# Spreading the dequantisation of packed 4-bit weights over the set-up of a transformer-block kernel

## The chip, the core and the metric

The kernel runs on one core of a Trainium2 chip. The metric is the device time in microseconds (us) of one execution. Before the change it is 905.2 us, the median of 3 runs (905.16 to 906.35).

The names used below: PE is TensorE, DVE is VectorE, ACT is ScalarE, POOL is GpSimd, SP is SyncE (here only a queue that issues DMAs). L985 is line 985 of the kernel.

## What is computed

One block on `x` of 32 x 64 tokens, 512 wide:

```python
# layer norm, cross attention of x on ctx with 16 heads of 4 x 8 channels,
# channels mixed by a 4x4 matrix per head, scores per channel group m
qh = interfere(proj(ln(x), Wq, bq)); kh, vh = the same of ctx with Wk, Wv
w  = softmax(einsum('bhqdm,bhkdm->bhqkm', qh, kh) / sqrt(8), axis=3)
x  = x + einsum('bhqkm,bhkdm->bhqdm', w, vh).reshape(...) @ Wo.T + bo
# feed forward with 4-bit weights: 8 values per uint32, groups of 128 rows
W[i, j] = scale[g[i], j] * (nibble[i, j] - (zero[g[i], j] + 1))
h  = silu(ln(x) @ W_gate) * (ln(x) @ W_up)       # 512 -> 1376
x  = x + h @ W_down                              # 1376 -> 512
```

`g` is an input (one group number per row), 4 groups for gate and up, 10 for down. Everything is kept in pairs of 16-bit numbers: a high half and a low half with the rest, so that a product is three matmuls.

## The kernel before, in words

Tokens are taken in 8 chunks of 256. The loop body runs the attention of chunk c and, between its steps, slices of the feed forward of chunk c-1. There are 20 places ("slots") for such slices in a chunk: two ahead of the scores, four in each of four batches, four at the tail. The order of work on each engine is written out by hand (`pe_chunk`, `act_chunk`, `dve_chunk`, `pool_chunk`), and the engines meet at semaphores. An engine works its own list strictly in order.

Chunk 0 has no feed forward of a chunk before, so its slots hold the dequantisation of the feed-forward weights, which stay in SBUF from then on. Chunk 1 can't start its slices before the last unit is done (`d_lo`).

**Set-up** (`sync_setup`, `pe_setup`, `act_setup`, `dve_setup`, `pool_setup`). A small matrix per weight block is built from `interference` (DVE, to L972). PE turns the biases with it (L403, L406) and folds it into Wk, Wv, Wq (L420); Wo is put in another column order by 32 copies on DVE (L985) and turned on PE (L423). ACT brings the folded weights back to SBUF (L737). DVE takes the largest absolute value of each weight (L988), of the scales (L994, L995) and of the eight chunks of context (L998). POOL takes the maximum over all partitions (`partition_all_reduce`, L1297), DVE works out scale factors from it, powers of two, up to L1045 (`scale_ready`). Then ACT and DVE write the high (`act_whi`, L749) and low (`dve_wlo`, L1059) halves of the four weights, and keys, values and queries of chunk 0 are projected. POOL makes the one-hot matrices of the group numbers (`pool_hot`, L1320 to L1324) and the rests of the scale tables (L1301 to L1310); ACT rounds those tables (L758), DVE unpacks the zero points (`dve_zeros`, L1067, L1070).

**A unit of the dequantisation** is a block of 128 rows by up to 512 columns; there are ND = 35 (24 of gate and up, 16 of them 512 and 8 of them 352 columns wide, and 11 of down). Unit n goes through

1. DVE: shift and mask the nibbles, SBUF to SBUF (`dve_dequant_int`, L1083),
2. ACT: convert to bf16 (`act_dequant_conv`, L794),
3. PE: three matmuls; scale rows into PSUM bank UB (L443), minus the zero rows (L444) plus the nibbles (L446) into bank GB,
4. ACT: GB times a power of two into SBUF (`act_dequant_scaled`, L777),
5. DVE: that times UB (`dve_dequant_w`, L1094),
6. ACT: the high half (`act_dequant_hi`, L767), 7. POOL: the low half (`pool_dequant_lo`, L1334).

Matmuls of unit n wait for step 5 of unit n-1, since there is one pair of banks:

```python
reached(e, S["d_w"], n)
```

The packed weights come in 14 pieces of up to 688 KB over two buffers; a piece is loaded when the units of the piece two before it are through step 1.

Of the kernel before, what the change touches and what calls it, by code (L numbers as in the profile page):

```python
# [22 lines left out]
P = 128  # L23
# [60 lines left out]
TICKS = ND + 3  # L84
FIRST_SLOT = 2
TICK_ENDS = [0] * FIRST_SLOT + [TICKS * (k + 1) // (SLICES - FIRST_SLOT) for k in range(SLICES - FIRST_SLOT)]

def ticks(slot):
    return range(TICK_ENDS[slot - 1] if slot else 0, TICK_ENDS[slot])  # L90

# [12 lines left out]
def build(nc, x, ctx_in, Wq, bq, Wk, bk, Wv, bv, interference, amp, Wo, bo,  # L104
          qw_gu, qz_gu, sc_gu, gi_gu, qw_d, qz_d, sc_d, gi_d, out):
    with ExitStack() as stack:
# [16 lines left out]
        small = sb("small", [P, 124], F32)  # L123
# [66 lines left out]
        wop = [take(2048, F32) for _ in range(KB)]  # L190
        bvx = take(2048, F32)

        inter_all, inter_own, own = wop[0][:, 0:HEADS * SUP * SUP], wop[1][:, 0:HEADS * SUP * SUP], wop[2][:, 0:4 * SUP]
# [20 lines left out]
        scgu = words(WD_f, 2 * INTER, 2 * INTER)  # L214
        o = [0]

        def temp(n):
            o[0] += n
            return words(WGU_f, o[0] - n, n)
        rest_gu, rest_d, scd = temp(2 * INTER), temp(DM), temp(DM)  # L220
        zint = temp(2 * INTER).bitcast(U32)
        zraw_gu, zraw_d = temp(2 * INTER // 8).bitcast(U32), temp(DM // 8).bitcast(U32)
        gidx_gu, gidx_d, hot_f = temp(DM), temp(INTER), temp(INTER)
# [23 lines left out]
        BMASK = small[:, 108:124].rearrange("p (w v k) -> p w v k", w=2, v=2)  # L247
        GM = small[:, 100:101]
# [6 lines left out]
            "const_loaded", "bo_loaded", "sc_loaded", "gi_loaded", "z_loaded", "qw_loaded0", "qw_loaded1",  # L255
# [5 lines left out]
            "sc_high", "sc_rest", "hot_ready", "z_ready",  # L261
# [53 lines left out]
        def sync_chunk(e, c, first=False):  # L315
            if first:
                load_ctx(e, 1)
            if not is_last(c):
                e.wait_ge(S["xres_ready"], 2 * c + 2)
                e.wait_ge(S["xln_ready"], 2 * c + 2)  # L320
                e.dma_start(xin, x_d[c + 1]).then_inc(S["x_loaded"], 16)
            reached(e, S["pv_done"], SLOTS * c)
            v_dmas(e, c, first)
            if first:
                for i in range(2, len(PIECES)):
                    e.wait_ge(S["d_int"], units_before(i - 1))
                    load_piece(e, i)
# [18 lines left out]
        def sync_setup(e):  # L346
# [5 lines left out]
            e.dma_start(zraw_gu[0:GROUPS_GU, :], qz_gu).then_inc(S["z_loaded"], 16)  # L352
            e.dma_start(zraw_d[0:GROUPS_D, :], qz_d).then_inc(S["z_loaded"], 16)
            for w in WORDER:
                e.dma_start(wraw[w], (Wq, Wk, Wv, Wo)[w].rearrange("(g p) n -> p g n", p=P)).then_inc(S[f"w_loaded{w}"], 16)
                if w == WORDER[0]:
                    e.dma_start(gidx_gu[0:96, :].bitcast(I32), gi_gu.partition_broadcast(96)).then_inc(S["gi_loaded"], 16)
                    e.dma_start(gidx_d[0:96, :].bitcast(I32), gi_d.partition_broadcast(96)).then_inc(S["gi_loaded"], 16)

            e.wait_ge(S["sc_zeroed"], 1)  # L360
            for i in range(PARTS):
                e.dma_start(scgu[32 * i:32 * i + GROUPS_GU, :], sc_gu).then_inc(S["sc_loaded"], 16)
                e.dma_start(scd[32 * i:32 * i + GROUPS_D, :], sc_d).then_inc(S["sc_loaded"], 16)

            for c in range(NCHUNK):
                e.dma_start(cmax_st[:, c].rearrange("p (t n) -> p t n", t=TILES), c_d[c]).then_inc(S[f"ctxm_loaded{c}"], 16)
            e.dma_start(cin, c_d[0]).then_inc(S["ctx_loaded"], 16)
            e.dma_start(xin, x_d[0]).then_inc(S["x_loaded"], 16)
            load_piece(e, 0)
            load_piece(e, 1)  # L370
            e.dma_start(bo_row[:, :], bo.partition_broadcast(P)).then_inc(S["bo_loaded"], 16)

# [24 lines left out]
        def pe_setup(e):  # L397
            e.wait_ge(S["t_ready"], 2)
            e.wait_ge(S["pool_const"], 1)

            for i in range(2):
                for g in range(KB):
                    mm = e.matmul(bank[4][:, 4 * i + g:4 * i + g + 1], tmat[:, g, :], BQR[:, 4 * i + g:4 * i + g + 1],  # L403
                                  start=True, stop=True)
            for g in range(KB):
                mm = e.matmul(bank[5][:, g * P:(g + 1) * P], bvx[:, g * P:(g + 1) * P], tmat[:, g, :],  # L406
                              start=True, stop=True)
            mm.then_inc(S["bias_done"], 1)
            for i, w in enumerate(WORDER):
                banks = bank[4 * (i % 2):4 * (i % 2) + 4]  # L410
                e.wait_ge(S[f"w_loaded{w}"], 16)
                reached(e, S["fold_evicted"], i - 1)
                if i == 1:
                    e.wait_ge(S["bias_evicted"], 1)
                if w == 3:
                    e.wait_ge(S["wo_permuted"], 1)
                for cb in range(KB):
                    for g in range(KB):
                        if w < 3:
                            mm = e.matmul(banks[cb][:, g * P:(g + 1) * P], wraw[w][:, g, cb * P:(cb + 1) * P],  # L420
                                          tmat[:, g, :], start=True, stop=True)
                        else:
                            mm = e.transpose(banks[cb][:, g * P:(g + 1) * P], wop[g][:, cb * P:(cb + 1) * P], ident[:, :])  # L423
                mm.then_inc(S["fold_done"], 1)

        def pe_dequant(e, n):
# [6 lines left out]
            pick = slice(blk * P, blk * P + m)  # L436
            if n == 0:
                e.wait_ge(S["hot_ready"], 2)
                e.wait_ge(S["z_ready"], 2)
                e.wait_ge(S["sc_high"], 6)  # L440
                e.wait_ge(S["ident16_ready"], 1)
            reached(e, S["d_w"], n)
            e.matmul(UB[0:m, 0:cols], hot[0:64 + groups, pick], sc3[0:64 + groups, c0:c0 + cols], start=True, stop=True)  # L443
            e.matmul(GB[0:m, 0:cols], hot[0:groups, pick], z[0:groups, c0:c0 + cols], start=True, stop=False)  # L444
            e.wait_ge(S["d_conv"], n + 1)
            e.matmul(GB[0:m, 0:cols], ident16[0:m, 0:m], wbf[n % 2][0:m, 0:cols], start=False, stop=True).then_inc(S["d_gathered"], 1)  # L446

        def t_bank(c, name):

            if isinstance(c, int) and c < 0:  # L450
                return {"cT0": AB[2], "cT1": AB[3], "xT0": GB, "xT1": UB}[name]
# [81 lines left out]
        def pe_chunk(e, c, first=False, last=False):  # L533
# [4 lines left out]
            def ffn_slice(k):  # L538
                if first:
                    for n in ticks(k):  # L540
                        pe_dequant(e, n - 1)
# [7 lines left out]
            if first:  # L549
                e.wait_ge(S["fold_evicted"], 4)  # L550
                for t in range(TILES):
                    pe_transpose_tile(e, -1, f"cT{t}", cin, S["ctx_loaded"], 16)
# [5 lines left out]
            if first:  # L558
                e.wait_ge(S["wlo_done"], 2)
                for t in range(TILES):  # L560
                    pe_rows(e, 2, t, AB[2 + t], cxT, S["proj_done"])
                for i in range(TILES):
                    pe_transpose_tile(e, -1, f"xT{i}", xln, S["xln_ready"], i + 1)
                e.wait_ge(S["wlo_done"], 3)
                e.wait_ge(S["t_lo"], t_at(-1, "xT1"))
            else:
# [162 lines left out]
        def act_setup(e):  # L729
            e.wait_ge(S["bias_done"], 1)  # L730
            e.activation(bv_row[:, :], bank[5][:, :], ACT.Copy)
            e.activation(bqk[:, :, :].rearrange("p a b -> p (a b)"), bank[4][:, 0:8], ACT.Copy).then_inc(S["bias_evicted"], 1)
            for i, w in enumerate(WORDER):
                e.wait_ge(S["fold_done"], i + 1)
                e.wait_ge(S["wmax_done"], i + 1)
                for cb in range(KB):
                    ins = e.activation(wraw[w][:, cb], bank[4 * (i % 2) + cb][:, :], ACT.Copy)  # L737
                ins.then_inc(S["fold_evicted"], 1)
                if i == 1:
                    act_scale_part(e, 0)  # L740
# [3 lines left out]
            act_whi(e, 1)  # L744

# [5 lines left out]
        def act_scale_part(e, i):  # L751

            if i == 0:
                e.wait_ge(S["sc_loaded"], 32 * PARTS)
            else:
                e.wait_ge(S["sc_rest"], 2 * i)
# [723 lines left out]
```

## Time and profile before

| | |
|---|---|
| median of 3 runs | 905.2 us |
| the profiled execution | 906.32 us, of which the core's span in the profile is 904.6 us |
| set-up, to the first scores of chunk 0 | 0 to 108.8 us of the span |
| chunk 0 from its scores to the first matmul of the next chunk | 108.8 to 240.3 us |
| the other seven chunks and the last feed forward | 240.3 to 904.6 us |
| PE busy | 85% of the span |
| DVE, ACT, POOL busy | 56%, 48%, 36% |

A row of a timeline gives the start, the time taken, the engine, the line, the operation, what it writes and reads, the shapes, and in brackets the idle time of the engine ahead of it with what ended it. Neighbouring instructions of a line are merged (x32), their time then is from the first's start to the last's end.

### The profile page before, as it was taken

To read this page: it belongs to the slowest core of one execution; us is meant where nothing else is said; L and a number is where in the kernel's file an instruction comes from. 1 tells how busy PE (TensorE), PEld (TensorE's weight loads), DVE (VectorE), ACT (ScalarE), POOL (GpSimd) and SP (SyncE) were. 2 spreads that over 40 slices of the span, in tenths; PEclk is the share of its full clock that TensorE was granted. 3 is DMA by queue.
4 is the path that set the end of the run, shared out by engine and by line. 5 is a ranking of instruction groups with operands and counts; after the bars stand their busy time and mean duration, and the time that the engine had idled before them with its cause. 6 is when DMAs were issued, how large, how long until landed. Compare 5 with 4: busy or idle time off the path is not lost.

```text
span 904.6 us, 23874 instructions
## 1 busy us (share of the span) xinstructions
PE 772.6 (85%) x9953; PEld 562.3 (62%) x9953; DVE 510.2 (56%) x1013; ACT 438.3 (48%) x806; POOL 326.8 (36%) x290
## 2 busy tenths in 40 slices
PE   5306457766799999999999999999999999999898
PEld 5303323322278857876787778677857885787484
DVE  6987745554465646655574556456645663644421
ACT  1426355676365526662555455454635462655120
POOL 6732324555314530543064114412431352144220
PEclk9758655565599999999999999999999999999999
DMA  8900113222101011002100110011001100010000
GB/s 248 292 23 1 50 32 89 69 56 63 32 25 28 3 49 50 3 3 71 28 2 14 60 28 3 13 60 28 2 21 52 28 2 25 3 27 3 24 1 23
DMA packets 20702, 36.98 MB, mean 41 GB/s; under 512 B 3374, under 2 KB 7602, under 8 KB 20592
## 3 DMA queue, kind: packets, MB, share of 16 engines
q1 hardware_dynamic: 20604, 35.48, 13.5%
q8 instruction: 85, 1.39, 0.6%
q14 instruction: 13, 0.11, 0.0%
HBM read 26.56 MB, written 4.19 MB: 34 GB/s over the span
## 4 chain that ended last, share of the span: by engine, by line
PE 67%; DVE 15%; ACT 8%; issue 6%; DMA 2%; SPq 1%; DVEq 0%; ACTq 0%; POOL 0%
PE bank L511 16%; PE bank L526 13%; PE bank L482 9%; PE bank L492 9%; PE bank L644 4%; DVE nmf L1166 4%; PE bank L638 3%; PE bank L661 3%; ACT arena L849 3%; PE bank L619 2%; PE bank L459 2%; DVE arena L1094 2%; DMA arena<-in_L_xattn_Wo 2%; DVE arena L985 2%; PE bank L443 2%
## 5 line engine op out<-in xcount | busy, mean ns | idle before, releaser
L511 PE MATMUL bank<-arena,WGU 128*128 128x256 f16 (+1 forms) x2112 | 247.0, 274 | 1.4 <-DVE arena L709 1.4
L511 PEld LDWEIGHTS bank<-arena,WGU 128*128 128x128 f16 (+1 forms) x2112 | 206.2, 100 | 27.5 <-DVE arena L709 1.6
L1368 POOL TENSOR_TENSOR arena<-arena 128x512 f16<-128x512 f32 x128 | 147.0, 1173 | 190.5 <-ACT arena L856 190.5
L482 PE MATMUL bank<-arena,WT 128*128 128x256 f16 x768 | 91.3, 281 | 40.4 <-DVE arena L709 39.1
L526 PE MATMUL bank<-WD,arena 128*128 128x512 f16 (+1 forms) x528 | 121.1, 379 | 0.0
L849 ACT ACTIVATE arena<-bank,small 128x512 f32<-128x512 f32 x128 | 89.1, 776 | 58.3 <-PE bank L644 58.3
L1355 POOL TENSOR_TENSOR arena<-arena 128x512 f16<-128x512 f32 (+1 forms) x48 | 51.7, 1077 | 172.2 <-ACT arena L829 172.2
L482 PEld LDWEIGHTS bank<-arena,WT 128*128 128x128 f16 x768 | 76.9, 101 | 54.6 <-issue 43.1
L492 PE MATMUL bank<-WT,arena 128*128 128x512 f16 x384 | 88.0, 387 | 1.8 <-DVE arena L707 1.8
L526 PEld LDWEIGHTS bank<-WD,arena 128*128 128x128 f16 (+1 forms) x528 | 49.4, 98 | 53.2
L1166 DVE TENSOR_REDUCE nmf<-bank 128x8 f32<-128x512 f32 x128 | 79.4, 682 | 4.4 <-PE bank L619 4.2
L809 ACT ACTIVATE arena<-bank,bqk,small 128x256 f32<-128x256 f32 x64 | 38.4, 601 | 82.2 <-PE bank L482 82.2
L856 ACT ACTIVATE arena<-arena 128x512 f16<-128x512 f32 x128 | 71.9, 628 | 0.0
L813 ACT ACTIVATE arena<-bank,small 128x256 f16<-128x256 f32 x128 | 67.9, 608 | 0.0
L492 PEld LDWEIGHTS bank<-WT,arena 128*128 128x128 f16 x384 | 38.0, 99 | 47.4 <-issue 4.2
L1118 DVE SCALAR_TENSOR_TENSOR arena<-arena,small 128x512 f16<-128x512 f32 x64 | 45.2, 748 | 37.5 <-ACT arena L813 37.5
L644 PE MATMUL bank<-nmT,sel 32*128 32x128 f32 x1024 | 61.6, 317 | 0.0
L1125 DVE RECIPROCAL rinv<-bank 128x16 f32<-128x16 f32 x64 | 16.3, 255 | 78.1 <-PE bank L661 78.1
L1341 POOL TENSOR_TENSOR rstd<-vareps,small 128x1 f32<-128x1 f32 x32 | 19.6, 622 | 100.2 <-DVE vareps L1104 93.1
L1146 DVE SCALAR_TENSOR_TENSOR arena<-arena,small,bank 128x512 f32<-128x512 f32 (+1 forms) x48 | 33.6, 699 | 38.3 <-PE bank L511 37.1
L1142 DVE SCALAR_TENSOR_TENSOR arena<-arena,bank 128x512 f32<-128x512 f32 (+1 forms) x48 | 30.7, 639 | 41.9 <-ACT arena L825 41.9
L661 PEld LDWEIGHTS bank<-arena 128*128 128x128 f16 x1536 | 46.9, 97 | 9.7 <-issue 1.8
(157 smaller groups left out, 1068.8 us busy)
## 6 DMA issues: line engine op xcount, KB each, us to landing
arena<-in_L_ffn_qweight_gu SPq DMA_DIRECT2D x8, 688.0 KB, 5.4
arena<-arena SPq DMA_DIRECT2D x32, 144.0 KB, 3.0
WT<-in_ctx SPq DMA_DIRECT2D x8, 512.0 KB, 15.1
arena<-in_ctx SPq DMA_DIRECT2D x8, 512.0 KB, 3.7
arena<-in_x SPq DMA_DIRECT2D x8, 512.0 KB, 3.6
out_y<-arena SPq DMA_DIRECT2D x16, 256.0 KB, 2.1
arena<-in_L_ffn_qweight_down SPq DMA_DIRECT2D x10, 256.0 KB, 3.4
arena<-in_L_xattn_Wk SPq DMA_DIRECT2D x1, 1024.0 KB, 6.6
```

The costliest lines, as they stand in the source:

```text
L482: mm = e.matmul(jb[:, g2 * TOK:(g2 + 1) * TOK], WT[:, w, sp, kb, g * P:(g + 1) * P], src[:, mp, kb, :], start=(n == 0), stop=(n == 11))
L492: mm = e.matmul(jb[:, :], src[:, sp, kb, t * P:(t + 1) * P], WT[:, w, mp, kb, :], start=(n == 0), stop=(n == 11))
L511: mm = e.matmul(pb[0:m, i * TOK:(i + 1) * TOK], WGU[:, sp, kb, half * INTER + fb * P:half * INTER + fb * P + m], x2T[:, mp, kb, :], start= ...
L526: mm = e.matmul(pb[:, :], hT[0:m, sp, fb, t * P:(t + 1) * P], WD[0:m, mp, fb, :], start=(n == 0), stop=(n == 3 * FB - 1))
L644: mm = e.matmul(AB[a][:, i * P:(i + 1) * P], sel[rows, i, :], nmT[rows, :], start=False, stop=True)
L661: mm = e.matmul(JB[0][:, at:at + 2 * VCOLS], phl[:, a, part, i * P:(i + 1) * P], vv[:, b, :, 4 * i + a, v0:v0 + VCOLS], start=(n == 0), st ...
L813: ins = e.activation((qm, km)[w][:, 0, NB * g:NB * g + NB, v, :], src.rearrange("p (n t) -> p n t", n=NB), ACT.Identity, bias=BMASK[:, w, ...
L849: e.activation(pring[:, a, :], AB[a][:, :], ACT.Exp, bias=LIFT, scale=KSM).then_inc(S["exp_done"], 1)
L856: e.activation(phl[:, a, 0, :], pring[:, a, :], ACT.Copy).then_inc(S["p_hi"], 1)
L1166: e.tensor_reduce(nmf[:, a, 0:8], AB[a][:, :].rearrange("p (n k) -> p n k", n=8), AX_X, ALU.max, negate=True).then_inc(S["max_done"], 1)
L1355: e.tensor_tensor(flat(1), hbuf[0:m, u % 2, 0:cols], flat(0), ALU.subtract).then_inc(S["h_lo"], 1)
L1368: e.tensor_tensor(phl[:, a, 1, :], pring[:, a, :], phl[:, a, 0, :], ALU.subtract).then_inc(S["p_lo"], 1)
```

## The change

- The dequantisation starts in the set-up. Instead of two units or so in each of 18 slots, the steps are spread over named places: 26 ticks in 15 places of the set-up and ahead of the scores, and 14 in the slots of chunk 0, three in each batch and two at the tail.
- Units below 23 with an even number use a second pair of PSUM banks (JB), so their matmuls wait for step 5 of unit n-2. The folds of the weights then have one set of four banks, where they had two in turn.
- Step 2, the conversion to bf16, moves from ACT to POOL. Step 5 is three ticks behind step 1, where it was one.
- The tables of gate and up are made wide (128 and 32 partitions in place of 4) on DVE and sent to their rows by 12 and 4 small DMAs. Their one-hot matrix is made on DVE, that of down stays on POOL in four parts between the folds.
- The maximum over the scales gets a `partition_all_reduce` of its own, early.
- The 32 copies that reorder Wo go from DVE to ACT.
- The loads are put in another order: pieces of packed weights between the weights and the chunks of context, each behind a wait on step 1.

```diff
+PLACES = ["tables", "bias", "fold0", "fold1", "fold2", "fold3", "ctx2", "ctx4", "ctx6", "ctx8", "scales", "w0", "w1",
+          "keys", "values"] + list(range(SLICES))
+TICKS_AT = {"tables": 2, "bias": 2, "fold0": 2, "fold1": 2, "fold2": 2, "fold3": 2, "ctx2": 1, "ctx4": 1, "ctx6": 1,
+            "ctx8": 1, "scales": 2, "w0": 2, "w1": 2, "keys": 2, "values": 2}
+BATCH_TICKS = [slot[j] for slot in IN_BATCH for j in (0, 2, 3)] + AT_TAIL[:2]
+TWO_PAIRS = sum(TICKS_AT[p] for p in PLACES[:PLACES.index("values") + 1]) - 3
...
@@ def sync_setup
+            load_piece(e, 0)
+            load_w(e, 1)
...
+            load_piece(e, 1)
+            e.wait_ge(S["sc_zeroed"], 2)
+            e.wait_ge(S["wide_ready"], 1)
+            for i in range(PARTS):
+                for g in range(GROUPS_GU):
+                    e.dma_start(sc3_gu[32 * i + g:32 * i + g + 1, :], sc3w[32 * g:32 * g + 32, i, :]).then_inc(S["sc_table"], 16)
+            e.wait_ge(S["zwide_ready"], 1)
+            for g in range(GROUPS_GU):
+                e.dma_start(z_gu[g:g + 1, :], zw[8 * g:8 * g + 8, :]).then_inc(S["z_table"], 16)
+            load_w(e, 2), load_w(e, 0)
+            load_next_piece(e, 2)
+            load_w(e, 3)
+            load_ctx_max(e, 0), load_ctx_max(e, 1)
+            load_next_piece(e, 3)
...
+        def pe_ticks(e, place):
+            for n in ticks(place):
+                pe_dequant(e, n - 2)
+        def dq_banks(n):
+            return (JB[0], JB[1]) if n < TWO_PAIRS and n % 2 == 0 else (GB, UB)
@@ def pe_dequant
-            reached(e, S["d_w"], n)
+            reached(e, S["d_w"], n - 1 if n < TWO_PAIRS else n)
@@ def act_setup
             for i, w in enumerate(WORDER):
+                if w == 3:
+                    act_permute(e)
                 e.wait_ge(S["fold_done"], i + 1)
                 e.wait_ge(S["wmax_done"], i + 1)
...
+                act_ticks(e, f"fold{i}")
+            for place in ("ctx2", "ctx4", "ctx6", "ctx8"):
+                act_ticks(e, place)
+            act_scale_part(e, 2)
+            act_ticks(e, "scales")
             e.wait_ge(S["scale_ready"], 1)
             act_whi(e, 0)
             act_hi(e, -1, "cT0"), act_hi(e, -1, "cT1")
+            act_ticks(e, "w0")
             act_whi(e, 1)
+            act_ticks(e, "w1")
+        def act_ticks(e, place):
+            for n in ticks(place):
+                act_dequant_scaled(e, n - 2)
+                act_dequant_hi(e, n - 4)
@@ def dve_setup
+            dve_tables(e)
+            dve_ticks(e, "tables")
             link(e, e.tensor_copy(T1, smalli[:, 4:5]))
...
+        def dve_tables(e):
...
+            e.wait_ge(S["maxq_all"], 1)
...
+        def dve_ticks(e, place):
+            for n in ticks(place):
+                dve_dequant_int(e, n)
+                dve_dequant_w(e, n - 3)
@@ def pool_setup
-            pool_hot(e, GROUPS_D, INTER, gidx_d, hot_d)
-            pool_hot(e, GROUPS_GU, DM, gidx_gu, hot_gu)
+            e.wait_ge(S["maxq_ready"], 1)
+            e.partition_all_reduce(MRQ, MXQ, P, ABSMAX).then_inc(S["maxq_all"], 1)
...
+            pool_ticks(e, "tables")
+            pool_ticks(e, "bias")
+            for i in range(4):
+                pool_hot_d(e, i)
+                pool_ticks(e, f"fold{i}")
...
+            for place in ("ctx2", "ctx4", "ctx6"):
+                pool_ticks(e, place)
             e.wait_ge(S["max_ready"], 1)
             e.partition_all_reduce(MR, MX, P, ABSMAX).then_inc(S["max_all"], 1)
+            pool_ticks(e, "ctx8")
             pool_ln(e, "x", 0)
+            pool_ticks(e, "scales")
...
+        def pool_ticks(e, place):
+            for n in ticks(place):
+                pool_dequant_conv(e, n)
+                pool_dequant_lo(e, n - 5)
+        def pool_dequant_conv(e, n):
...
+            e.wait_ge(S["d_int"], n + 1)
+            reached(e, S["d_gathered"], n - 1)
+            e.tensor_copy(wbf[n % 2][0:m, 0:cols], wint[n % 2][0:m, 0:cols]).then_inc(S["d_conv"], 1)
```

Step 1 of unit n still waits for the conversion of unit n-2 (`d_conv`), as before.

## Rows read from the trace of the kernel before

**Rows 1.** Busy time of each engine by stretch, with the granted clock

```profile
core 0: us, PE busy (x) PEld busy (x) DVE busy (x) ACT busy (x) POOL busy (x), PEclk, DMA share, GB/s
...
108.80:240.30 131.50, 82.76 (x838) 38.81 (x838) 69.17 (x129) 80.84 (x149) 58.09 (x53) 0.56 0.22 59
```

**Rows 2.** Timeline of DVE in the set-up

```profile
22.19 14.38 DVE L985 COPY arena<-arena 128x64 f32<-128x64 f32 x32 [1.35 <-DMA arena<-in_L_xattn_Wo]
36.49 2.27 DVE L988 TENSOR_REDUCE maxima<-arena 128x1 f32<-128x2048 f32 x1
...
42.93 9.08 DVE L998 TENSOR_REDUCE small<-WT 128x1 f32<-128x1024 f32 x8
...
59.43 0.49 DVE L1045 TENSOR_SCALAR bv_row<-bv_row,small 128x512 f32<-128x512 f32 x1
...
88.19 6.77 DVE L1191 TENSOR_TENSOR arena<-arena 128x512 f16<-128x512 f32 x2
```

**Rows 3.** Chain that ended last, 108.8 to 240.3 us: shares, then start, time, piece

```profile
by line: DVE arena L1094 11.7%; PE bank L443 10.7%; ACT arena L777 10.2%; PE bank L446 10.0%; PE bank L444 9.6%; DVE nmf L1166 7.2%; issue 6.7%; PE bank L644 6.5%; ACT arena L849 4.5%; PE bank L638 4.3%; DVE arena L1083 3.4%; PE bank L619 3
...
231.19 0.70 ACT arena L777
...
234.37 0.70 ACT arena L777
```

**Rows 4.** Timeline of POOL in the set-up

```profile
4.36 2.41 POOL L1293 MEMSET WD<- 96x2752 f32 x1
...
19.56 3.11 POOL L1322 TENSOR_TENSOR WGU<-WGU 96x1376 f32<-96x1376 f32 x1
22.76 4.86 POOL L1323 TENSOR_SCALAR WGU<-WGU 96x1376 f32<-96x1376 f32 x1
27.72 3.82 POOL L1324 TENSOR_SCALAR arena<-WGU,small 96x1376 bf16<-96x1376 f32 x1
31.61 0.64 POOL L1320 CAST WGU<-WGU 96x512 f32<-96x512 int32 x1
...
60.00 1.12 POOL L1341 TENSOR_TENSOR rstd<-vareps,small 128x1 f32<-128x1 f32 x2 [7.14 <-issue]
```

**Rows 5.** Single lines: shortest, median and longest duration in ns

```profile
L985 DVE COPY arena<-arena x32: 195/202/4866, 22.2 to 36.4; 128x64 f32<-128x64 f32 x32
...
L1083 DVE TENSOR_SCALAR arena<-arena,smalli x35: 394/486/1474, 112.7 to 233.4; 128x512 uint32<-128x512 uint32 x26, 128x352 uint32<-128x352 uint32 x8, 96x512 uint32<-96x512 uint32 x1
...
L1059 DVE SCALAR_TENSOR_TENSOR WT<-arena,small,WT x4: 2335/2352/6647, 62.0 to 84.5; 128x2048 f16<-128x2048 f32 x4
```

**Rows 6.** Groups by line, 0 to 215 us: busy us, mean ns of one, idle before

```profile
L1334 POOL TENSOR_TENSOR WGU<-arena,WGU 128x512 f16<-128x512 f32 (+1 forms) x24 | 27.0, 1136 | 48.1 <-ACT WGU L767 48.1
L777 ACT ACTIVATE arena<-bank,small 128x512 f32<-128x512 f32 (+1 forms) x27 | 17.5, 650 | 23.3 <-PE bank L446 23.3
L1094 DVE TENSOR_TENSOR arena<-arena,bank 128x512 f32<-128x512 f32 (+1 forms) x27 | 17.2, 636 | 31.9 <-ACT arena L777 31.9
L446 PE MATMUL bank<-arena,ident 128*128 128x512 bf16 (+1 forms) x28 | 14.9, 532 | 0.0
...
L749 ACT ACTIVATE WT<-arena,small 128x2048 f16<-128x2048 f32 x4 | 8.1, 2020 | 17.5 <-DVE bv_row L1045 17.5
```

**Rows 7.** Timeline of PE: starts of its stages

```profile
9.05 3.57 PE L403 MATMUL bank<-small,arena 128*128 128x1 f32 x16 [9.05 <-DVE arena L972]
...
14.33 11.94 PE L420 MATMUL bank<-arena 128*128 128x128 f32 x96
...
96.30 8.11 PE L482 MATMUL bank<-arena,WT 128*128 128x256 f16 x48 [12.57 <-DVE arena L709]
108.80 1.47 PE L619 MATMUL bank<-arena 32*128 32x128 f16 x48 [4.38 <-DVE arena L1118]
...
240.29 7.79 PE L492 MATMUL bank<-WT,arena 128*128 128x512 f16 x24 [1.77 <-DVE arena L707]
```

**Rows 8.** Timeline of SP's queue: the issue of one load

```profile
12.21 0.29 SPq L362 DMA_DIRECT2D WD<-in_L_ffn_scales_gu  x1
```

More of the change, by code:

```diff
@@ L83, with ticks @@
 PARTS = 3
[L84 to L90, printed above, removed]
+TICKS = ND + 5
+PLACES = ["tables", "bias", "fold0", "fold1", "fold2", "fold3", "ctx2", "ctx4", "ctx6", "ctx8", "scales", "w0", "w1",
[3 more added lines that the diff above has]
+BATCH_TICKS = [slot[j] for slot in IN_BATCH for j in (0, 2, 3)] + AT_TAIL[:2]
+assert sum(TICKS_AT.values()) + len(BATCH_TICKS) == TICKS
+TICKS_AT.update((k, 1) for k in BATCH_TICKS)
+TWO_PAIRS = sum(TICKS_AT[p] for p in PLACES[:PLACES.index("values") + 1]) - 3
+def ticks(place):
+    before = sum(TICKS_AT.get(p, 0) for p in PLACES[:PLACES.index(place)])
+    return range(before, before + TICKS_AT.get(place, 0))
 def width(block):
@@ L189, in build @@
         eye4 = take(16, F32)
+        early = [take(2048, F32) for _ in range(KB)]
+        bvx = take(2048, F32)
+        inter_all, inter_own, own = early[0][:, 0:HEADS * SUP * SUP], early[0][:, 256:512], early[1][:, 0:4 * SUP]
+        zraw_d = early[1][:, 4 * SUP:4 * SUP + DM // 8].bitcast(U32)
+        zint_d, scd = early[2].bitcast(U32), early[3]
+        rest_d = take(2048, F32)
         wop = [take(2048, F32) for _ in range(KB)]
-        bvx = take(2048, F32)
-        inter_all, inter_own, own = wop[0][:, 0:HEADS * SUP * SUP], wop[1][:, 0:HEADS * SUP * SUP], wop[2][:, 0:4 * SUP]
         take, pos = carver(max(pos[0], body0_end))
@@ L247, in build @@
         BMASK = small[:, 108:124].rearrange("p (w v k) -> p w v k", w=2, v=2)
+        MXQ, MRQ, BDQ, SCQ = (small[:, 124 + 2 * i:126 + 2 * i] for i in range(4))
         GM = small[:, 100:101]
@@ L539, in ffn_slice @@
                 if first:
-                    for n in ticks(k):
-                        pe_dequant(e, n - 1)
+                    pe_ticks(e, k)
                     return
@@ L833, in act_slot @@
             if first:
-                for n in ticks(k):
-                    act_dequant(e, n)
+                act_ticks(e, k)
             else:
@@ L869, in act_chunk @@
                 act_whi(e, 2)
+                act_ticks(e, "keys")
             else:
@@ L1155, in dve_slot @@
             if first:
-                for n in ticks(k):
-                    dve_dequant_int(e, n)
-                    dve_dequant_w(e, n - 1)
+                dve_ticks(e, k)
             else:
@@ L1327, in pool_dequant_lo @@
+        def pool_dequant_conv(e, n):
+            if not 0 <= n < ND:
+                return
+            _, (blk, down, c0, cols) = DQ_UNITS[n]
+            m = width(blk) if down else P
+            e.wait_ge(S["d_int"], n + 1)
+            reached(e, S["d_gathered"], n - 1)
+            e.tensor_copy(wbf[n % 2][0:m, 0:cols], wint[n % 2][0:m, 0:cols]).then_inc(S["d_conv"], 1)
         def pool_dequant_lo(e, n):
@@ L1358, in pool_slot @@
             if first:
-                for n in ticks(k):
-                    pool_dequant_lo(e, n - 3)
+                pool_ticks(e, k)
             else:
@@ L1370, in pool_chunk @@
         def pool_chunk(e, c, first=False, last=False):
+            if first:
+                pool_ticks(e, "keys")
+                e.wait_ge(S["bo_loaded"], 16)
+                e.wait_ge(S["wlo_done"], 3)
+                pool_xres(e, 0)
+                pool_ticks(e, "values")
             pool_slot(e, c, 0, first)
```

279 lines of the change are left out of this document (164 added, 115 removed).

## The prediction

> **What bounds the kernel now.** I read the busy times by stretch first. From 108.8 to 240.3 us the clock granted to PE is 0.56, its lower level of 1.2 GHz most of the time, and no engine is busy for two thirds of the stretch [rows 1]: a chain bounds it, not an engine. The chain of waits names it: steps 5, 3, 4 and 1 of the dequantisation (L1094, L443, L777, L446, L444, L1083) hold 55.6% of the stretch [rows 3], 73.1 us or 2.09 us for each of the 35 units. Where nothing else runs, a unit takes 3.18 us, from one L777 to the next [rows 3]. The other 58.4 us are chunk 0's own attention. The set-up ahead of it is bounded by DVE: from 22.2 us it reorders Wo (14.4 us), takes maxima until 52.0 us and has the scale factors at 59.9 us [rows 2]; the query projection starts at 96.3, the scores at 108.8 and the next chunk at 240.3 us [rows 7]. After that the change touches nothing, so it is worth what it moves the mark at 240.3 us.
>
> The third thing to see is how DVE and POOL get in each other's way. A copy of 202 ns (median) takes 4866 ns once [rows 5], and it lies beside POOL's L1323 of 4.86 us [rows 4]. L1059 takes 6.65 us once and else 2.35, L1083 0.49 and up to 1.47 us [rows 5]; L1191 takes 6.77 us for two [rows 2], where L1094 of the same size takes 0.64 each [rows 6]. Such a DVE operation waits until POOL's ends. Reductions don't show it. The 32 copies are 6.4 us of work and the rest is waiting.
>
> **What goes.** The attention of chunk 0 keeps 12 units of 35 (units 23 to 34). At 2.09 us each they are 25.1 us on its chain; 58.4 + 25.1 = 83.5 us in place of 131.5, so 48.0 us go. I checked the share: the tick ahead of the maximum's turn adds steps 1 and 5 and three matmuls, the last one of a batch waits for exponentials, step 4 and step 5, some 6 us a batch. The bounds are nothing on the chain (another 25.1 us gone) and 3.18 us each (13.1 us less gone). The middle is nearest to what the stretch shows.
>
> **What comes, stage by stage.** Prices: on PE a unit is three matmuls of 0.53, 1.6 us; on ACT steps 4 and 6 are 0.65 each, 1.3 us; on DVE steps 1 and 5 are 0.4 and 0.6, 1.0 us [rows 5, 6] without waiting; on POOL step 7 is 1.1 us [rows 6]. The conversion on POOL isn't in the trace. Its nearest row is the cast of 96x512 in 0.64 us; the bounds are that and the two-input operation of step 7, 1.14 us; I take 0.6 as a mean with the narrow units, so a tick is 1.7 us of POOL.
>
 The zero fills end near 5.6 us (L1293 is halved), a swap and the reduction end at 13.1, and the swap back at 20.2 us. DVE is held at `maxq_all` until 13.1, then has 2 us of factors and first ticks and the 4.8 us of matrices that stood ahead of L403; PE gets its bias matmuls at 20.2 us, not 9.05, and needs 5.3 us for them [rows 7]. Unit 0 is through step 5 at 25.5 + 1.6 + 0.65 + 0.65 = 28.4 us.
>
> *To the end of the context maxima.* DVE's work from there: four weight maxima of 2.28 us, 9.1 for the context [rows 2], 2.1 of small maxima and zero points, 11 ticks of 1.0: 31.3 us. Its waits: the one-hot matrix of down is four POOL operations of 4.9, 3.1, 4.9 and 3.8 us [rows 4], one at each fold. A step 1 (or the table cast) that comes behind their start waits 2.6, 1.9, 4.5 and 2.6 us by my laying out, and three more times it waits for a step 7 of 1.1; step 5 waits 0.8 us for ACT once and 4.9 us at the last fold, behind the reordering of Wo (32 small copies on ACT, 3 to 6.4 us, 5 taken, near the 202 ns of a copy on DVE [rows 5]), four more of PE's transposes and 2.1 of eviction. Together 20.6. The maxima end at 28.4 + 31.3 + 20.6 = 80.3 us, where they end at 52.0 now. The 14.4 us that DVE sheds are in this.
>
> *The scale factors.* POOL is done some 1.6 us before DVE, then swaps (7.1) and reduces (0.4): 86.2 us, 4 us after the layer-norm statistics of DVE that would cover it. The factors take 5.8 us (59.9 less 52.0, less 2.1 of statistics): 92.0 us, against 59.9.
>
> *To the query projection.* Now 36.4 us. Two waits of DVE for POOL go, since the operations behind them are gone: 4.3 (L1059) and 5.5 (L1191). Added: 3.7, since ACT's first high half stands behind unit 15, whose conversion waits for the swap back; 0.9 of L1059 behind a step 7; a pair of ticks at w0, 1.0 + 1.6 + 1.3 = 3.9; at w1 2.6 and the second weight's halves, 2.0 and 2.35 [rows 5, 6], which now stand ahead of PE's key projection, 7.0; at the keys 3.9 and a L1059 of 2.35, 6.2; at the values 2.0 + 1.6 + 1.3 and 1.2 of halves that were hidden, 6.1; and 1.5 for two-input operations of DVE that meet POOL. 36.4 - 9.8 + 29.3 = 55.9 us: the query projection starts at 147.9 us and the scores, 12.5 us later as now, at 160.4. That is 51.6 later.
>
> *At no cost.* The 16 table DMAs take SP about 0.3 us each [rows 8], 5 us, and hold back two weight loads that DVE wants after 35 us. Loads behind waits on step 1 (the last weight at 24 us, contexts from 24 to 64 us) each come over 5 us ahead of their maxima. If the first conversions slip by more than that, SP's queue is what is late next. One set of banks for the folds costs PE a wait for the eviction, which lies beside DVE's reduction.
>
> **Sum.** +51.6 and -48.0 give +3.6 us on the mark at 240.3 us. The profiled execution took 906.32 us, its span 904.6; the median is 905.2, 1.1 below that execution. 905.2 + 3.6 = 908.8 us. The change takes a chain of 3 us a unit away and puts in another of 2.2 us a unit, paced by POOL and DVE in turn.
>
> At two places the Trainium skill prices what I took from rows. GPSIMD Engine Reference, section 2.1, says that the first call after new code has been loaded pays about 6 us with no visible instruction. The row has 7.14; with 6 us on the three swaps that lie on the path, the sum would be near 905.4, no change. The same page, section 3.1, has 769 ns as its best case for 512 elements of one input; the row of the cast has 640, and with the page's figure on the 14 conversions that DVE waits for, the sum would be 2 us higher.
>
> **Rivals.** *A, as summed*, 900 to 917 us. *B, the waits of DVE for POOL are mostly missed.* Who comes first has the port: step 1 comes 0.4 us behind the 4.9 us operation at the third fold in my laying out, so a slip of half a microsecond turns 4.5 us to nothing, and it may free the steps behind. Without the 11.6 and 3.3 us of these waits it is 893.9 us. For it: DVE then runs two units ahead; against: POOL still has to come round, and L1083 waits often even with POOL under half busy. *C, slower: POOL paces the set-up more than laid out.* Place: conversions and swaps. If the conversion is 1.14 us, 14 on the path cost 7 us more; and the first two swaps fall in the time in which the loads are heaviest, where one now falls with nothing to show its length; 5 us for these. 920.8 us. It decides from a conversion of 0.9 us on. *D, the 12 units left are all exposed*, at 3.18 us: 921.9 us. For it: with one tick a slot each unit waits for a step on another engine's list; against: the exponentials and maxima cover some. That the early units aren't done early can't be: each engine's list forces it. That the second pair of banks does nothing is likely in part, and changes nothing in the sum, since POOL and DVE pace the ticks.
>
> **How the numbers follow.** A 0.38, B 0.32, C 0.20, D 0.10. Of A's 0.38, 0.08 lie below 903.4, 0.12 within 0.2% (1.8 us, what a measurement of this kernel can tell from no change) and 0.18 above. So faster 0.40, same 0.12, slower 0.48. The range reaches past B and C by the bounds of the conversion and the waits, 890 to 924; A's own is 900 to 917.
>
> **What would show it.** In the profile after: an idle of about 7 us on POOL ahead of the first conversion and twice around the second all-reduce; the conversion near 0.6 us; step 1 with a median above 0.5 us and some of 2 to 5 us in the folds; `scale_ready` near 92, the query projection near 148, the scores near 160 and the next chunk's first row matmuls near 244 us; 84 us of attention with 12 units. Wrong I am if the scores come before 150 us (B) or after 170 (C), or if the attention of chunk 0 takes 95 us (D) or 70.

## The result, and the profile after

The changed kernel takes 923.95 us (median of 4 runs, 923.25 to 924.24) against 905.47 us before (4 runs): ratio 1.0201, 95% interval 1.0184 to 1.0219. It is slower by 18.5 us. The forecast was 908.8 us, slower, in a range of 890 to 924. The result lies 0.05 us inside the upper end of that range and outside the 900 to 917 of the sum itself, where rival D stood with 921.9 us.

The busy times by stretch of the kernel after, cut at its first scores and at the first row matmuls of the next chunk, where [rows 1, 7] have 108.8 and 240.3 us:

```profile
core 0: us, PE busy (x) PEld busy (x) DVE busy (x) ACT busy (x) POOL busy (x), PEclk, DMA share, GB/s
0.00:162.30 162.30, 80.84 (x347) 47.87 (x348) 99.70 (x215) 65.28 (x134) 68.07 (x76) 0.71 0.43 121
162.30:257.60 95.30, 47.45 (x765) 30.28 (x765) 37.22 (x80) 37.69 (x68) 39.98 (x41) 0.57 0.07 20
257.60:922.50 664.90, 647.27 (x8844) 487.92 (x8844) 352.84 (x700) 316.20 (x598) 214.08 (x202) 0.99 0.08 23
```

The set-up is 53.5 us longer (162.3 for 108.8), chunk 0's attention 36.2 us shorter (95.3 for 131.5), and the rest 664.9 us where it was 664.3. So the change is worth what it moves the mark at 240.3 us, which is at 257.65 us now: 17.4 us of the 17.9 in the span. The clock in the attention is 0.57 in place of 0.56; it plays no part.

The timeline of DVE in the set-up after, for [rows 2]:

```profile
17.15 0.62 DVE L1051 COPY arena<-bv_row 128x128 f32<-128x128 f32 x4
...
27.36 7.23 DVE L1178 TENSOR_SCALAR arena<-arena 10x64 uint32<-10x64 uint32 x8
...
42.50 2.54 DVE L1194 TENSOR_SCALAR arena<-arena,smalli 128x512 uint32<-128x512 uint32 x1
...
52.10 4.13 DVE L1194 TENSOR_SCALAR arena<-arena,smalli 128x352 uint32<-128x352 uint32 x1
...
61.05 3.32 DVE L1194 TENSOR_SCALAR arena<-arena,smalli 128x352 uint32<-128x352 uint32 x1
72.31 0.52 DVE L1205 TENSOR_TENSOR arena<-arena,bank 128x352 f32<-128x352 f32 x1 [7.94 <-ACT arena L870]
...
82.24 2.34 DVE L1069 TENSOR_REDUCE small<-WT 128x1 f32<-128x1024 f32 x2
...
95.96 0.48 DVE L1120 TENSOR_SCALAR bv_row<-bv_row,small 128x512 f32<-128x512 f32 x1
```

Step 1 (L1194) takes 0.48 us (0.40 for 352 columns) where POOL is quiet and 2.5, 4.1 and 3.3 us behind three of the one-hot operations. Eight tiny operations on the zero points take 7.2 us behind the first; unhindered they took 0.93. The other side is the timeline of POOL after, for [rows 4]:

```profile
11.48 0.37 POOL L1405 PARTITION_ALL_REDUCE small<-small  x1 [5.89 <-issue]
20.30 1.14 POOL L1407 TENSOR_TENSOR arena<-arena 96x512 f32<-96x512 f32 x1 [8.45 <-issue]
22.17 1.17 POOL L1456 CAST arena<-arena 128x512 bf16<-128x512 uint32 x2 [0.73 <-ACT arena L849]
...
27.57 0.68 POOL L1456 CAST arena<-arena 128x512 bf16<-128x512 uint32 x1 [1.02 <-PE bank L510]
...
29.62 4.90 POOL L1440 TENSOR_SCALAR WD<-WD 96x1376 f32<-96x1376 f32 x1
37.76 0.61 POOL L1456 CAST arena<-arena 128x512 bf16<-128x512 uint32 x1 [3.23 <-DVE arena L1194]
...
41.66 3.10 POOL L1442 TENSOR_TENSOR WD<-WD 96x1376 f32<-96x1376 f32 x1
...
51.18 4.86 POOL L1444 TENSOR_SCALAR WD<-WD 96x1376 f32<-96x1376 f32 x1
...
89.81 0.43 POOL L1419 PARTITION_ALL_REDUCE maxima<-maxima  x1 [6.27 <-issue]
90.11 0.69 POOL L1456 CAST arena<-arena 128x512 bf16<-128x512 uint32 x1
97.87 1.15 POOL L1465 TENSOR_TENSOR WGU<-arena,WGU 128x512 f16<-128x512 f32 x1 [7.06 <-issue]
```

What the prediction calls the four swaps of code are the idle times put down to "issue" around the two all-reduces: 5.9 and 8.5, 6.3 and 7.1 us. The timeline of PE gives the marks after, for [rows 7]: the query projection (L546), the scores of the four batches (L683) and the next chunk's rows (L556):

```profile
150.94 6.86 PE L546 MATMUL bank<-arena,WT 128*128 128x256 f16 x48 [1.46 <-issue]
162.29 1.47 PE L683 MATMUL bank<-arena 32*128 32x128 f16 x48 [4.50 <-DVE arena L1229]
...
184.84 1.47 PE L683 MATMUL bank<-arena 32*128 32x128 f16 x48
...
209.24 1.47 PE L683 MATMUL bank<-arena 32*128 32x128 f16 x48
...
230.80 1.47 PE L683 MATMUL bank<-arena 32*128 32x128 f16 x48
...
257.65 7.64 PE L556 MATMUL bank<-WT,arena 128*128 128x512 f16 x22 [1.54 <-DVE arena L771]
```

A batch takes 22.6, 24.4 and 21.6 us. What stands at the end of the first one is read in the chain that ended last, from the end of its exponentials to the next scores:

```profile
176.78 0.27 ACT arena L870
...
177.23 0.51 ACT WGU L858
177.74 1.03 ACT arena L932 x2
178.78 0.59 ACT arena L763
179.39 0.75 DVE arena L773
180.14 0.60 DVE stats L1210
...
181.15 0.60 DVE stats L1210
...
182.09 0.49 DVE arena L1194
182.57 0.61 DVE arena L1205
...
183.23 0.61 PE bank L507
```

PE's three matmuls of the batch's last tick (from 183.23) wait for step 5 (L1205), which has its input since 177.4 us, but stands on DVE's list behind the low half of turned activations (L773), which itself waits for ACT, and behind the layer-norm statistics of the next chunk (L1210). The next scores stand behind those matmuls on PE's list.

### The profile page after: what moved, and what is told of

The parts are those of the page before. It is cut to its first block, busy times and chain, and to the rows that moved or that the text cites. A ratio compares the mean times of both kernels' runs of the same rounds, so it can differ in the third digit from the quotient of the medians.

```text
span 922.5 us, 23901 instructions
## 1 busy us (share of the span) xinstructions
PE 775.6 (84%) x9953; PEld 566.1 (61%) x9953; DVE 489.8 (53%) x995; ACT 419.2 (45%) x800; POOL 322.1 (35%) x319
## 3 DMA queue, kind: packets, MB, share of 16 engines
q1 hardware_dynamic: 21404, 35.48, 13.1%
## 4 chain that ended last, share of the span: by engine, by line
PE 66%; DVE 13%; ACT 8%; issue 8%; POOL 2%; SPq 2%; DMA 1%; DVEq 0%; ACTq 0%; POOLq 0%
PE bank L575 16%; PE bank L590 12%; PE bank L546 9%; PE bank L556 9%; PE bank L708 4%; DVE nmf L1275 4%; PE bank L725 3%; PE bank L702 3%; ACT arena L925 2%; PE bank L523 2%; PE bank L683 2%; DVE arena L1194 1%; DVE arena L1205 1%; DVE stats L1210 1%; PE bank L507 1%
## 5 line engine op out<-in xcount | busy, mean ns | idle before, releaser
L546 PE MATMUL bank<-arena,WT 128*128 128x256 f16 x768 | 90.2, 280 | 2.6 <-issue 2.5
L556 PE MATMUL bank<-WT,arena 128*128 128x512 f16 x384 | 90.0, 394 | 1.5 <-DVE arena L771 1.5
L546 PEld LDWEIGHTS bank<-arena,WT 128*128 128x128 f16 x768 | 76.6, 100 | 16.4 <-issue 5.6
L1275 DVE TENSOR_REDUCE nmf<-bank 128x8 f32<-128x512 f32 x128 | 79.4, 682 | 12.5 <-PE bank L683 12.3
L556 PEld LDWEIGHTS bank<-WT,arena 128*128 128x128 f16 x384 | 38.6, 101 | 49.0 <-issue 7.2
L870 ACT ACTIVATE arena<-bank,small 128x512 f32<-128x512 f32 (+2 forms) x35 | 23.2, 662 | 82.9 <-PE bank L510 64.0
L1456 POOL CAST arena<-arena 128x512 bf16<-128x512 uint32 (+2 forms) x35 | 20.6, 590 | 106.3 <-PE bank L510 71.3
L725 PE MATMUL bank<-arena 128*128 128x34 f16 x1536 | 50.0, 180 | 6.0 <-POOL arena L1498 6.0
```

Of the source, the lines that this page charges most:

```text
L546: mm = e.matmul(jb[:, g2 * TOK:(g2 + 1) * TOK], WT[:, w, sp, kb, g * P:(g + 1) * P], src[:, mp, kb, :], start=(n == 0), stop=(n == 11))
L556: mm = e.matmul(jb[:, :], src[:, sp, kb, t * P:(t + 1) * P], WT[:, w, mp, kb, :], start=(n == 0), stop=(n == 11))
L725: mm = e.matmul(JB[0][:, at:at + 2 * VCOLS], phl[:, a, part, i * P:(i + 1) * P], vv[:, b, :, 4 * i + a, v0:v0 + VCOLS], start=(n == 0), st ...
L1275: e.tensor_reduce(nmf[:, a, 0:8], AB[a][:, :].rearrange("p (n k) -> p n k", n=8), AX_X, ALU.max, negate=True).then_inc(S["max_done"], 1)
```

## The experiments

Three theories of the attention, where the forecast missed: (1) the order on the lists exposes the units left; (2) one unit in a slot exposes its own latency whatever the order; (3) the attention itself grew. And for the set-up: which of POOL's three new burdens (swaps, one-hot operations between the folds, conversions) costs what, and what the copies of Wo are worth alone. All runs below are beside runs of the kernel before on the same chip, 905.5 to 906.0 us. The changed kernel was not run again beside them; differences from it are taken from its 923.95 us, and one of 1 or 2 us can't be told from none.

### The last tick of a batch first on DVE's list (e3)

```diff
                 dve_slot(e, c, slot[2], first)
+                if first:
+                    dve_slot(e, c, slot[3], first)
                 for name in EXTRAS[b][1]:
...
-                dve_slot(e, c, slot[3], first)
+                if not first:
+                    dve_slot(e, c, slot[3], first)
```

> The changed kernel; in chunk 0 the last tick of each batch stands on DVE's list ahead of the turned halves, the layer-norm statistics and the layer-norm application of the next chunk, not behind them. Theory 1, the order on the lists exposes the units left in the attention: the next scores start 2.8 us earlier in batch 0, some 4 us in batch 1 and 0.7 us in batch 2, together 7 to 8 us (916). Theory 2, a unit per slot is exposed by its own latency of 3.2 us whatever the order: within 2 us of 924.

Measured: 911.45 us (910.43 to 912.34), 12.5 us less than the change. PE's timeline of this kernel has the scores of the four batches and the next chunk at:

```profile
161.93 1.47 PE L683 MATMUL bank<-arena 32*128 32x128 f16 x48 [4.50 <-DVE arena L1229]
...
179.38 1.47 PE L683 MATMUL bank<-arena 32*128 32x128 f16 x48
...
199.78 1.47 PE L683 MATMUL bank<-arena 32*128 32x128 f16 x48
...
220.00 1.47 PE L683 MATMUL bank<-arena 32*128 32x128 f16 x48
...
245.47 7.17 PE L556 MATMUL bank<-WT,arena 128*128 128x512 f16 x24 [1.54 <-DVE arena L771]
```

The batches take 17.5, 20.4 and 20.2 us, so 5.1, 4.0 and 1.3 us less, and the attention 83.5 us, 11.8 less. Theory 1 holds, and its effect is larger than I wrote. In the first batch step 5 now also stands ahead of L773 and no longer shares its wait for ACT.

### The units of the attention left out (e4)

In steps 1 to 5 the bound on the unit's number becomes 24, and pieces of packed weights from there on aren't loaded. So this kernel leaves out steps 1 to 5 of the 11 units 24 to 34, and the down weights are not computed; steps 6 and 7 of all units and step 5 of unit 23 stay in the attention.

```diff
-            if not 0 <= n < ND:
+            if not 0 <= n < STEPS:      # STEPS = 24, in five helpers
```

> The changed kernel without steps 1 to 5 of units 24 to 34 (their halves are made from what the buffers hold) and without the loads of their packed weights: the attention of chunk 0 nearly alone. If the 95.3 us from the first scores to the next chunk are 58 of attention and 37 of units (theories 1 and 2), they become 60 to 64 us and the run 890 to 893. If the attention itself became longer behind the new set-up (theory 3, by the clock or by POOL's steps), they stay above 70 us and the run above 900.

```profile
163.35 1.47 PE L686 MATMUL bank<-arena 32*128 32x128 f16 x48 [5.40 <-DVE arena L1232]
...
224.83 7.62 PE L559 MATMUL bank<-WT,arena 128*128 128x512 f16 x24 [1.54 <-DVE arena L774]
```

By PE's timeline the attention takes 61.5 us, so theory 3 falls: the attention nearly alone is close to what it was (58.4 us by the shares of [rows 3], without any step of a unit). The 11 units cost 95.3 - 61.5 = 33.8 us, 3.1 each. With the order of e3 they cost 83.5 - 61.5 = 22.0 us, 2.0 each. The run took 913.49 us (910.71 to 915.83), some 20 us more than expected. The mark of the next chunk is 32.8 us earlier and the span only 10.8: the later chunks are 22 us longer. The waits of PE from 300 to 800 us in this kernel have a first line that is small in the others:

```profile
PE bank L549 <- issue: 15.8, 9, 3.2
PE bank L696 <- DVE nmf L1278: 7.6, 10, 1.1
```

The wait for DVE is the same 7.6 us as in the changed kernel over 500 us of its own loop, but the projection of the queries (L549) waits nine times, 15.8 us in all and up to 3.2, for nothing that the profile shows, where the changed kernel has 1.0 us in all. The rest of the 22 us is a longer busy PE, 654.1 us for 647.3, at a granted clock of 0.98 in place of 0.99. Why an earlier part of the program with fewer instructions does that to a loop that is the same was not tried, and stays open. The mark, not the run's time, carries this experiment.

### One pair of banks (e2)

```diff
-TWO_PAIRS = sum(TICKS_AT[p] for p in PLACES[:PLACES.index("values") + 1]) - 3
+TWO_PAIRS = 0
...
-                e.wait_ge(S["d_w"], TWO_PAIRS)
+                e.wait_ge(S["d_w"], 23)
```

> The changed kernel with one pair of banks for all units. My sum has POOL and DVE pace the ticks of the set-up: within 2 us of 924. The rival, that PE and the banks pace them: each of the pairs of ticks in a place becomes a chain of 3.2 us, some 10 us more (934).

Measured: 940.72 us (935.17 to 941.67), 16.8 us more than with two pairs. Its query projection starts at 165.70 us in place of 150.94. The rival is right and I was wrong: the second pair is worth 17 us, and PE and its banks do pace the pairs of ticks. Ahead of the scale factors it gives 4.5 us (they end at 101.0 for 96.4), between them and the queries, where PE, ACT and DVE pass each unit on in turn, 10.2.

### The early all-reduce left out (e5)

```diff
-            e.partition_all_reduce(MRQ, MXQ, P, ABSMAX).then_inc(S["maxq_all"], 1)
+            e.memset(MRQ, 0.019).then_inc(S["maxq_all"], 1)
```

> The changed kernel with the early partition_all_reduce over the scales left out and a constant of 0.019 put in its place, which gives the same power of two; two of the four code swaps of POOL go. Theory: POOL's first conversion comes at 13 in place of 22 us and its one-hot operation no longer stands in front of DVE's table (7.2 us at 27 to 35 us), so the context maxima end some 6 us earlier and the run is 918. Rival: PE's bias matmuls, ready at 18 us, and the folds set the pace, and nothing moves (within 2 us of 924).

Measured: 922.45 us (920.39 to 924.53), 1.5 us less, no more than the runs scatter. Both idle times of POOL are gone: it goes on at 8.92 us, and the first two conversions are at 13.1 in place of 22.2 us. The context maxima still end at 83.4 for 84.6 us. The rival holds: 5.9 and 8.5 us of idle POOL in the first 20 us cost next to nothing, because the first matmuls wait for DVE's matrices (L1051) until 17.8 us, and until 18.4 in this run, and no unit goes before.

### The one-hot operations of down left out (e6)

```diff
-                pool_hot_d(e, i)
...
+            e.memset(hot_d[0:96, :], 0.0).then_inc(S["hotd_ready"], 1)
```

The one-hot matrix of down is zero here, so the down weights are not computed.

> The changed kernel without the four POOL operations of the one-hot matrix of down (a zero fill in their place), 16.7 us of POOL. Theory: DVE's waits behind them, 6.3, 2.1 and 3.6 us, go, and the fourth was hidden behind ACT's copies: the context maxima end 10 to 12 us earlier, the run is 912 to 914. Rival: PE and ACT, with the folds and the reordering of Wo, take over as the pace and 3 to 5 us are all there is (919 to 921).

Measured: 915.03 us (914.08 to 916.20), 8.9 us less. The maxima end at 75.7, for 84.6 us. By the rows above DVE's waits behind the first three of these operations are 12 us; they are gone in this run. Two things take part of it back: the early all-reduce comes later (POOL is idle for 8.1 us ahead of it, for 5.9), so that the first step 5 is 2.3 us later, and the last fold's wait for ACT is 10.0 us in place of 7.9. So most of the 12 us were on the path.

### The conversions back on ACT (e7)

```diff
@@ def act_ticks
                 act_dequant_scaled(e, n - 2)
                 act_dequant_hi(e, n - 4)
+                act_dequant_conv(e, n)
@@ def pool_ticks
-                pool_dequant_conv(e, n)
                 pool_dequant_lo(e, n - 5)
```

> The changed kernel with one part undone: the conversions back on ACT, behind steps 4 and 6 of a tick. Theory, POOL's conversions cost little and save ACT's list: 5 to 10 us slower (929 to 934), since ACT's list makes step 1 of the next units wait for folds and first halves. Rival, the conversions on POOL are what slows the set-up, through swaps and the port: 4 to 8 us faster (916 to 920).

Measured: 915.33 us (914.50 to 917.42), 8.6 us less: my theory falls, and the rival's figure holds. The timeline of DVE in this kernel:

```profile
22.94 6.12 DVE L1205 TENSOR_SCALAR arena<-arena,smalli 128x352 uint32<-128x352 uint32 x2 [5.28 <-ACT arena L860]
...
29.57 0.92 DVE L1189 TENSOR_SCALAR arena<-arena 10x64 uint32<-10x64 uint32 x8
...
75.80 2.33 DVE L1080 TENSOR_REDUCE small<-WT 128x1 f32<-128x1024 f32 x2
...
86.61 0.49 DVE L1131 TENSOR_SCALAR bv_row<-bv_row,small 128x512 f32<-128x512 f32 x1
```

And of POOL:

```profile
23.88 4.90 POOL L1450 TENSOR_SCALAR WD<-WD 96x1376 f32<-96x1376 f32 x1
```

The maxima end at 78.1 in place of 84.6 us, the factors at 87.1 in place of 96.4, and from there to the queries it is 55.9 us in place of 54.5. So all of the gain lies ahead of the factors. It is not that conversions stood behind the one-hot operations: in the changed kernel POOL is idle for 3.2, 2.1, 0.3 and 6.8 us ahead of the first conversion after each of them. The conversions stood ahead. Those of units 2 and 3 wait for PE (1.0 us in the row at 27.57), and the first one-hot operation starts behind them at 29.62 us, beside the zero points. Without them it starts at 23.88, holds up two operations of step 1 (6.12 us, for 1.12), in part while DVE would have waited 2.8 us for ACT anyway, and the zero points take 0.92 in place of 7.23 us. They end at 30.5 for 34.6 us. Some 2.4 us more are won by 49 us, where step 5 no longer waits 2.5 us for ACT. The last 2.8 us are POOL's way to the second all-reduce: its last operation ahead of it ends at 73.3 for 83.5 us, and DVE no longer waits 2.4 us for the result. A burden of ACT's list, where I expected the loss, shows only in the 1.4 us after the factors. This gain and that of e6 both contain the zero points' wait, so they would not add in full; the two edits were not run together.

### The copies of Wo, in either kernel (e8, e1)

e8 is the changed kernel with the 32 copies back on DVE, at the last fold, in the form of the kernel before.

> The changed kernel with one part undone: the 32 copies of Wo back on DVE, at the last fold. Theory, in the changed kernel the copies on ACT (6.6 us) only shift a wait, since DVE stands idle for 7.9 us there: within 3 us of 924. Rival, the port: the copies stand behind POOL's one-hot operation of 3.9 us and DVE's list is longer by 6.4 us, 5 to 10 us slower (929 to 934).

Measured: 923.75 us (921.51 to 925.15), the same as the change. In the changed kernel the copies on ACT (6.55 us) only move the wait: DVE stands idle for 7.9 us behind them (the row at 72.31 above), and in e8, with 9.1 us of copies of its own, for 2.9.

e1 is the other half, the kernel before with this part of the change alone:

```diff
@@ def act_setup (kernel before)
             for i, w in enumerate(WORDER):
+                if i == 3:
+                    e.wait_ge(S["w_loaded3"], 16)
+                    ... the 32 copies, as e.activation(..., ACT.Copy)
+                    ins.then_inc(S["wo_permuted"], 1)
```

> The kernel before with one part of the change alone: the 32 copies that reorder Wo go from DVE to ACT. Two theories of what bounds the set-up. DVE's own work does: DVE sheds 14.4 us ahead of the context maxima, which end near 38 us in place of 52, and the run is some 14 us shorter (891). The loads do as soon as DVE is lighter: the last chunks of context land near 46 to 48 us, the maxima end near 48 to 49 us, and the run is 3 to 4 us shorter (902).

Measured: 893.06 us (892.24 to 893.45), ratio 0.9858 (0.9842 to 0.9874) to the kernel before. It beats both kernels. Its timelines of DVE and POOL:

```profile
29.89 9.08 DVE L999 TENSOR_REDUCE small<-WT 128x1 f32<-128x1024 f32 x8
...
42.45 0.69 DVE L1100 BATCH_NORM_STATS2 stats<-arena 128x6 f32<-128x512 f32 x1 [3.28 <-DMA arena<-in_x]
...
52.74 2.35 DVE L1060 SCALAR_TENSOR_TENSOR WT<-arena,small,WT 128x2048 f16<-128x2048 f32 x1 [2.07 <-ACT WT L759]
```

```profile
44.43 0.43 POOL L1298 PARTITION_ALL_REDUCE maxima<-maxima  x1 [5.75 <-issue]
```

The context maxima end at 39.0, 13 us earlier. The loads don't take over there, as the second theory had it; they do after it, with x at 42.4 us, and so does the swap, which the long wait used to hide. The factors end at 50.7 us, 9.2 earlier. The other 4.3 us are a meeting that moved: the first low half (L1060 here) takes 2.35 us, where it took 6.65 beside POOL in the kernel before (L1059, [rows 5]). The second one takes 6.17 us instead, and the key projection, 13.5 us earlier, doesn't wait for it. The next chunk starts at 226.78 us, 13.5 us earlier. A second set of runs, with this text ahead of it, gave the same:

> The kernel before with the copies of Wo on ACT, a second time beside its variant with the order of the lists: 893, as before.

892.80 us (892.41 to 893.18).

### Both repairs, in the kernel before and in the change (e9, e10)

> The kernel before with the copies of Wo on ACT, and in chunk 0 the last ticks of each batch ahead of the turned halves, the statistics and the layer norm on DVE. Theory 1: with two units in the last slot of a batch too, PE's matmuls stand behind those operations and ahead of the next scores: 3 to 8 us shorter than with the copies alone (885 to 890). Rival: with two units in each slot the chain of 3.2 us a unit hides the other operations of DVE, within 1.5 us of 893.

The edit is that of e3, on top of e1. Measured: 893.93 us in the median, 891.42 to 898.20, against 892.80 in the second runs of e1. PE's timeline has the first scores and the next chunk at:

```profile
100.18 1.47 PE L619 MATMUL bank<-arena 32*128 32x128 f16 x48 [4.50 <-DVE arena L1119]
...
231.57 7.07 PE L492 MATMUL bank<-WT,arena 128*128 128x512 f16 x24 [1.77 <-DVE arena L707]
```

The attention takes 131.4 us, for 131.5 in the kernel before. The rival holds: with two units in each slot nothing is to be had from the order. This is the execution of 898.20 us, and what it has more lies ahead of the scores, where the first low half takes 7.58 us beside POOL again. So some 5 us hang on a meeting that falls on the first low half in this execution and in neither profile of e1. The other four runs of e9, 891.42 to 894.04 us, suggest that it didn't there either, which no profile shows.

> The changed kernel with both repairs the runs point to: conversions on ACT (8.6 us less alone) and the last tick of a batch first on DVE's list (12.5 us less alone). They lie in different stages and should add: 903, no more than even with before. If 903, the change's plan is at best even, and the copies of Wo are all that it has to give.

The edits are those of e3 and e7 together. Measured: 907.01 us (10 runs, 903.06 to 909.91), ratio 1.0012 (0.9996 to 1.0028) to before: no difference that can be told. Of 21.1 us that the two took alone, 17 add: with the conversions on ACT the order is worth 8.2 us of attention (94.0 to 85.8), not 11.8. The mended plan is even with the kernel before and 14 us behind that kernel with the copies moved. What the rest of the plan costs the set-up, with the ticks themselves, the wide tables and the order of the loads, no experiment takes apart.

## Why the prediction was right, and which step of it was not

- **The number** was in the range by luck. The sum was 15 us short, the result 0.05 us inside the upper end, and by the prediction's own sign ("if the attention of chunk 0 takes 95 us (D)") the sum was wrong.
- **What bounds it** held: a chain in the attention, DVE's list in the set-up, DVE's waits behind POOL's operations. The rest of the run didn't move (664.9 us for 664.3).
- **The set-up** was laid out nearly as it came. To the end of the context maxima I had 80.3 us and it took 84.6; to the factors 92.0 and 96.4; to the queries 147.9 and 150.9; to the scores 160.4 and 162.3. So +51.6 us forecast and +53.5 measured. Within it, the term of the small waits was mis-sized: the zero points waited 6.3 us, not 2.6, the last fold's wait was 7.9 us, not 4.9, with copies of 6.55 us, not 5, and two other waits for ACT were 1.3 and 2.5 us, not 0.8. DVE's hold at `maxq_all` was 0.6 us and PE had its bias matmuls at 17.8, not 20.2 us, which took a part of that back. The conversion was priced at 0.6 us with a mean of 590 ns measured.
- **The attention** is the step that failed: "58.4 + 25.1 = 83.5 us" took 95.3 us. The layout priced a unit at the 2.09 us that it has with two units in a slot, and it was 3.1 us (e4). What stood in its place: the last unit of a batch stands on DVE's list behind the low half of the turned activations and the layer-norm work. e3 takes exactly this away, 11.8 us, and the attention is then 83.5 us, the figure forecast, with 2.0 us a unit. I had listed steps 4 and 5 for that tick and had left out what stands ahead of step 5 on DVE's own list. That a second unit in the slot covers this work in the kernel before fits e9, where the same edit moves nothing, but no run shows the cover itself. Rival D, at 0.10, had the price, 3.18 us; its mechanism, that each unit is exposed by its own wait, holds for no more than what e3 leaves.
- **Rival B** had a point: the waits of DVE for POOL cost about 9 us, but they were not missed; e6 had to take them away. **Rival C** fell in its mechanism (conversion 0.59 us, early swaps 1.5 us), though the conversions on POOL do cost 8.6 us: not by their length, but by when they let the one-hot operations and the second all-reduce start.
- **The second pair of banks** "changes nothing in the sum": wrong by 17 us. My layout had the pair in it from the start, and so the sum of the set-up was right where the sentence was not.
- **The table DMAs** were 0.3 us each in my price and 0.63 in the profile (12 in 7.57 us, 4 in 2.73); the two weights behind them still came early enough, so nothing followed.

The rule on new code of POOL (the Trainium skill, GPSIMD Engine Reference, section 2.1: about 6 us) agrees with the idle time ahead of an all-reduce, 5.9, 6.3 and, in e1, 5.75 us, though e6 has 8.1 once; behind one it is longer, 7.1 and 8.5 in the change. By e5 the early two don't bear on the time, where my layout had them on the path. The page's best case of 769 ns for 512 elements (section 3.1) is above the 0.61 us that a conversion of 512 took here.

## What to carry to other kernels

When work is spread thinner over a list of slots, ask for each slot what stands ahead of it on the same engine's list: a second unit in the slot may have been the cover. Look for the part of a large change that moves a block off the bounding engine, and run it alone: here one of seven parts gave 13 us on the kernel before and nothing inside the change, and the whole change stands 31 us behind that part alone. And an operation's place in an in-order list can cost more than its length: conversions of 0.6 us that wait for another engine held back an operation of 4.9 us until it met DVE's work, and cost 8.6 us in all.

## What the runs showed of the hardware

- A small DVE operation that meets a long one of POOL ends when POOL's does: 0.4 us becomes 4.13 beside L1444 of 4.86 us, and eight operations of 0.12 us become 7.23. A reduction of 2.27 us that runs beside L1444 for its last microsecond, and one wholly beside POOL's operations in [rows 2] (at 36.49), keep their 2.27.
- Which operation meets POOL's can differ between executions: the first low half of the weights took 6.65 us in the kernel before, 2.35 in both profiles of e1 (where the second took 6.17 and 7.27) and 7.58 in that of e9, with nothing changed ahead of it since e1.
- The idle time of POOL behind an all-reduce was 6.8 to 8.1 us for the one over the maxima, over all profiles, and 8.5 to 9.3 for the early one of the changed kernels, 6.8 in e6. Without the early all-reduce (e5) neither idle time is there. A conversion still ran right behind the second all-reduce, at 90.11 us, and only the operation after it waited; I had expected the first one to.
- In e4 the loop over the later chunks, unchanged in itself, was some 22 us longer, with 15.8 us in nine waits put down to nothing. The cause is open.
